# A four-layer graph network on one core: adjacency flag taken earlier, unit matrix from VectorE, weight preparation cut into four steps, output bias and the last norms on VectorE

## The reference, cut to what matters

```
L0: Wh = x W^T; e = leaky_relu(s1_i + s2_j), masked by adj == 0; softmax(e) @ Wh
L1: h = x W; logits = Ax_j + Ay_i + h a12 h^T; leaky_relu, masked by adj > 0; softmax @ x
    elu(x W1 + (softmax @ x) W2)
L2: 4 heads; q, k, v = x W + b; mask = adj | eye; softmax(q k^T * scale) @ v; relu(out @ Wo + bo)
L3: relational graph convolution over relation numbers 1 to 40: relu(sum_r (adj == r) @ ((h + b_r) * sigmoid(g + bg_r)))
```

## Time and profile before

| | |
|---|---|
| median of 3 runs | 518.59 us (518.09 to 518.69) |
| the profiled execution's own time | 518.74 us |
| its span, first to last instruction | 516.9 us |
| PE, PEld, DVE, ACT, POOL busy | 478.7, 411.4, 397.7, 425.1, 317.7 us |

### The profile page before, as it was taken

How to read it: one execution, slowest core, us unless ns; L and a number is a source line. 1 busy time by engine, 2 the same in 40 slices (tenths; PEclk the granted TensorE clock), 3 DMA queues, 4 the chain that set the end, 5 groups by cost and what they waited for, 6 DMA issues and landing times. The chain is left out here.

```text
span 516.9 us, 14050 instructions
## 1 busy us (share of the span) xinstructions
PE 478.7 (93%) x3964; PEld 411.4 (80%) x3964; DVE 397.7 (77%) x1558; ACT 425.1 (82%) x1261; POOL 317.7 (61%) x717
## 2 busy tenths in 40 slices
PE   3767899999999999999999999999999999999880
PEld 2556788888888898888888888888888888888660
DVE  3486788889888888889888888888987888766540
ACT  2444999989988888999898888898998988898740
POOL 3054456566766766666666676766676676664562
PEclk9988999999999999999999999999999999999996
DMA  6121101122122211222122221122212200000111
GB/s 188 30 83 41 42 13 53 53 63 61 55 63 62 62 44 37 58 63 63 52 64 62 63 58 31 49 63 62 63 52 64 62 23 22 22 22 22 32 32 30
DMA packets 40220, 26.92 MB, mean 52 GB/s; under 512 B 2641, under 2 KB 39889, under 8 KB 40146
## 3 DMA queue, kind: packets, MB, share of 16 engines
q1 hardware_dynamic: 40146, 26.03, 17.4%
HBM read 17.63 MB, written 8.39 MB: 50 GB/s over the span
## 5 line engine op out<-in xcount | busy, mean ns | idle before, releaser
L744 ACT ACTIVATE p<-p,nmax 128x256 f32<-128x256 f32 x256 | 126.6, 498 | 0.4 <-DVE nmax L941 0.4
L1140 POOL TENSOR_SCALAR x<-y,minus_mean,rstd 128x128 f32<-128x128 f32 x256 | 114.7, 458 | 17.7 <-issue 15.9
L1122 POOL TENSOR_TENSOR rstd<-ve,minus_half 128x2 f32<-128x2 f32 x128 | 101.9, 796 | 0.0
L941 DVE CUSTOM_DVE_ANT_0 p<-ps,neg 128x256 f32<-128x256 f32 x256 | 92.7, 419 | 6.6 <-PE ps L520 6.6
L1115 POOL TENSOR_SCALAR ve<-stats 128x2 f32<-128x2 f32 x128 | 24.7, 193 | 110.8 <-DVE stats L854 105.6
L753 ACT COPY p2T<-ps 128x512 f32<-128x512 f32 x128 | 75.0, 595 | 0.0
L531 PE MATMUL ps<-ident,p 128*128 128x128 f32 x512 | 71.7, 273 | 1.5 <-ACT p L744 1.5
L531 PEld LDWEIGHTS ps<-ident,p 128*128 128x128 f32 x512 | 57.4, 141 | 3.2 <-DVE nmax L941 1.4
L977 DVE SCALAR_TENSOR_TENSOR y<-ps,x 128x256 f32<-128x256 f32 x32 | 13.7, 427 | 56.6 <-PE ps L576 56.6
L854 DVE BATCH_NORM_STATS2 stats<-y 128x6 f32<-128x256 f32 x128 | 53.2, 415 | 2.3
L662 ACT COPY xT<-ps 128x256 f32<-128x256 f32 x96 | 36.6, 382 | 17.6 <-PE ps L400 17.1
(11 more groups left out here) (134 smaller groups left out, 1232.3 us busy)
## 6 DMA issues: line engine op xcount, KB each, us to landing
adj_in<-in_adj_dram SPq DMA_DIRECT2D x32, 256.0 KB, 3.0
xT<-in_xT_dram SPq DMA_DIRECT2D x32, 128.0 KB, 2.8
x_in<-in_x_dram SPq DMA_DIRECT2D x32, 128.0 KB, 3.0
x_aside<-x SPq DMA_DIRECT2D x32, 128.0 KB, 2.2
out_dram<-x SPq DMA_DIRECT2D x32, 128.0 KB, 1.8
l_w<-in_l_w_dram SPq DMA_DIRECT2D x1, 257.0 KB
l_w<-in_l_w_dram SPq DMA_DIRECT2D x1, 256.0 KB
first_w<-in_first_w_dram SPq DMA_DIRECT2D x1, 129.0 KB, 2.2
```

Source lines behind the costliest of these rows:

```text
L744: last = nc.scalar.activation(p2(n)[:, k, a, :], p2(n)[:, k, a, :], ACT.Exp, bias=nmax2(n)[:, k, a:a + 1], scale=-1.0, accum_out=sum2(n)[: ...
L941: last = nc.vector.tensor_tensor_reduce(p2(n)[:, k, a, :], bank("sc2", n, a)[:, k * N:(k + 1) * N], neg2(n)[:, k, :], -1.0, HIGHEST, ALU.a ...
L1122: nc.gpsimd.tensor_tensor(rstd[layer](n), ve[layer](n), minus_half[:, :], ALU.pow)\
L1140: last = nc.gpsimd.tensor_scalar(dst[:, k, 0:D], y_t[layer](n)[:, k, :], minus_mean[layer](n)[:, k:k + 1], rstd[layer](n)[:, k:k + 1], ALU ...
```

## The change

- DVE makes `ident`: a row of numbers 0 to 127 from eight memsets and four additions, a product on TensorE that spreads it, and a comparison. `lift` follows on DVE, `not_eye` on POOL from `ident`. The zero rows are cleared on POOL.
- `setup_later` is cut into `prep_a` to `prep_d` (TensorE) and `c_prep_a` to `c_prep_d` (ScalarE), with places of their own. `tT(0)`, `xw1(0)` wait for their results.
- `load` on SP is cut into `ld_xT`, `ld_adj`, `ld_w`, `ld_x`; the weights come ahead of graph 1.
- `bo` is added by DVE: `y2` becomes `y2a` (bank + `bo_row`) and `y2b` (relu and residual). The bf16 products of `wo2` and `setup_biases` are gone.
- `masks` is cut into `masks` (L0) and `neg1`. For the last three graphs, norms 2 and 3 are done on DVE (`end_norm2`, `end_norm3`).
- The flag is computed after `eq1(31)`: DVE `flag_a`, a product with ones on TensorE (`flag`), DVE `flag_b`. POOL's reduction is gone.
- All places in `PLAN` are new: `proj0` at 10694 and `agg3` at 17075 are 6.4 rounds apart. Ring `adj` 3 to 5, `eq1` 8 to 7.

```diff
 PLAN (new; steps of TensorE, ScalarE and GpSimd, and DVE)
+    "tensor": [("proj0", 10694), ("s2_rows", 10909), ("prep_a", 11545), ("pT0", 11559), ("prep_c", 11587),
+        ("agg0", 11591), ("prep_b", 11950), ("prep_d", 12017), ("xT1", 12109), ("tT", 12346), ("z1", 12576),
+        ("pT1", 12901), ("xw1", 13189), ("agg1", 13331), ("xT2", 13690), ("qk2", 13768), ("sc2", 13807),
+        ("pT2b1", 14236), ("v2", 14366), ("pT2a0", 14532), ("pT2b0", 14535), ("pT2a1", 14544), ("rs_rows", 14853),
+        ("agg2", 15034), ("wo2", 15329), ("xT3", 16364), ("hg3", 16806), ("agg3", 17075), ("flag", 15122)],
+    "scalar": [("c_proj0", 10868), ("c_s2", 11052), ("exp0", 11297), ("c_prep_a", 11621), ("c_pT0", 11639),
+        ("c_prep_c", 11695), ("c_prep_d", 12090), ("c_xT1", 12144), ("c_tT", 12315), ("relu1", 12724),
+        ("c_prep_b", 12783), ("exp1", 12944), ("c_pT1", 13008), ("c_xw1", 13181), ("c_elu1", 13268),
+        ("c_xT2", 13773), ("c_qk2", 13848), ("exp2b", 14128), ("exp2a", 14255), ("c_v2", 14440), ("c_pT2a0", 14693),
+        ("c_pT2b0", 14740), ("c_pT2a1", 14787), ("c_pT2b1", 14809), ("c_rs", 14944), ("c_xT3", 16481),
+        ("gate3", 16914)],
+    "vector": [("neg1", 10631), ("masks", 10935), ("e0", 11223), ("m0", 11295), ("s0", 11682), ("r0", 11806),
+        ("y0", 11811), ("b0", 11917), ("e1", 12655), ("r1", 13388), ("h1", 13390), ("y1a", 13403), ("y1b", 13415),
+        ("b1", 13501), ("e2b", 14087), ("e2a", 14161), ("r2", 14456), ("eq1", 14622), ("onT2", 15244),
+        ("y2a", 15378), ("y2b", 15614), ("b2", 15828), ("end_norm2", 16267), ("vals3", 17028), ("y3", 17318),
+        ("b3", 17955), ("end_norm3", 18990), ("flag_a", 14623), ("flag_b", 15622)],
+    "gpsimd": [("var0", 11827), ("rsq0", 11921), ("norm0", 12075), ("neg2", 13292), ("var1", 13386), ("rsq1", 13489),
+        ("norm1", 13573), ("rs_rep", 14785), ("var2", 15915), ("rsq2", 16034), ("norm2", 16145), ("var3", 18247),
+        ("rsq3", 18331), ("norm3", 19216)],
 DVE, setup
+                for k in range(8):
+                    last = nc.vector.memset(index[:, k:k + 1], float(k))
+                for k, size in enumerate((8, 16, 32, 64)):
+                    last = nc.vector.tensor_scalar(index[:, size:2 * size], index[:, 0:size], float(size), None, ALU.add)
+                nc.vector.tensor_tensor(ident[:, :], index[:, :], ps[:, 3, 0:P], ALU.is_equal)\
 TensorE
+                pe.matmul(ps[:, 3, 0:P], index[0:1, :], ones_row[:, :], start=True, stop=True)\
 wo2 and y2
-                    pe.matmul(o[:, k * D:(k + 1) * D], onT(n)[:, k * P:(k + 1) * P], l2_w[:, WO],
-                              start=True, stop=False)
-                    last = pe.matmul(o[:, k * D:(k + 1) * D], ones_bf[:, :], bo_parts[:, :],
-                                     start=False, stop=True)
+                    last = pe.matmul(o[:, k * D:(k + 1) * D], onT(n)[:, k * P:(k + 1) * P], l2_w[:, WO],
+                                     start=True, stop=True)
-                nc.vector.scalar_tensor_tensor(out=y_t[2](n), in0=o, scalar=0.0, in1=x2(n)[:, :, 0:D], op0=ALU.max, op1=ALU.add)\
+                nc.vector.tensor_tensor(y_t[2](n), o, bo_row[:, :].rearrange("p (t d) -> p t d", t=1)
+                                        .to_broadcast([P, T, D]), ALU.add).then_inc(sem("y2a_ready"), 1)
+                nc.vector.scalar_tensor_tensor(out=y_t[2](n), in0=y_t[2](n), scalar=0.0, in1=x2(n)[:, :, 0:D],
+                                               op0=ALU.max, op1=ALU.add).then_inc(sem("y2_ready"), 1)
 the end
-            pool.wait_ge(sem("excess_ready"), 1)
-            nc.gpsimd.partition_all_reduce(excess_all[:, :], excess_max[:, :], P, bass.bass_isa.ReduceOp.max)\
-                .then_inc(sem("excess_all_ready"), 1)
```

More of the change, by code:

```diff
@@ L26 @@
 PLAN = {
-    "sync": [("load", -56), ("aside", 7895), ("store", 10433)],
[15 rows of a table removed]
+    "sync": [("ld_xT", 9787), ("ld_adj", 10173), ("ld_w", 10463), ("ld_x", 11423), ("aside", 16293),
+        ("store", 18816)],
[6 rows of a table added]
+        ("c_prep_c", 11695), ("c_prep_d", 12090), ("c_xT1", 12144), ("c_tT", 12315), ("relu1", 12724),
[12 rows of a table added]
 }
 RING = {
[1 row of a table removed]
[1 row of a table added]
     "x1": 3, "xT1": 2, "tT": 2, "xw1": 3, "relu": 2, "p1": 2, "p1T": 2, "h": 2, "hexp": 2,
@@ L51 @@
 }
-FIRST_BANK = {"a": 0, "b": 4}
-WEIGHTS_AFTER = 0
+BANKS = {"a": (0, 1, 2, 3), "b": (4, 5, 6, 7)}
+AT_END = 3
+GRAPHS = {
+    **{step: (0, 1) for step in ("ld_w", "prep_a", "prep_b", "prep_c", "prep_d",
+                                 "c_prep_a", "c_prep_b", "c_prep_c", "c_prep_d")},
+    **{step: (-1, 0) for step in ("flag_a", "flag", "flag_b")},
+    **{step: (0, -AT_END) for step in ("norm2", "norm3")},
+    **{step: (-AT_END, 0) for step in ("end_norm2", "end_norm3")},
+}
 PSUM_USES = {
@@ L79 @@
     "agg2": [("b", "onT_sb")],
-    "wo2": [("b", "y2_ready")],
+    "wo2": [("b", "y2a_ready")],
     "xT3": [("b", "xT_sb3")],
@@ L83, with graphs_of @@
     "agg3": [("b", "y3_ready")],
-}
+    "prep_a": [], "prep_b": [], "prep_c": [], "prep_d": [],
+    "flag": [("b", "flag_ready")],
+}
+def graphs_of(step, graphs):
+    first, end = GRAPHS.get(step, (0, 0))
+    return range(first if first >= 0 else graphs + first, end if end > 0 else graphs + end)
 def program(engine, graphs):
@@ L90, in program @@
             sorted((place + 1000 * n, k, name, n)
-                   for k, (name, place) in enumerate(PLAN[engine]) for n in range(graphs))]
+                   for k, (name, place) in enumerate(PLAN[engine]) for n in graphs_of(name, graphs))]
 def psum_table(graphs):
-    table, rings = {}, {r: [] for r in FIRST_BANK}
+    table, rings = {}, {r: [] for r in BANKS}
     for step, n in program("tensor", graphs):
         for k, (ring, *_) in enumerate(PSUM_USES[step]):
-            uses = rings[ring]
-            table[step, n, k] = (FIRST_BANK[ring] + len(uses) % 4, uses[-4] if len(uses) >= 4 else None)
+            uses, banks = rings[ring], BANKS[ring]
+            table[step, n, k] = (banks[len(uses) % len(banks)],
+                                 uses[-len(banks)] if len(uses) >= len(banks) else None)
             uses.append((step, n, k))
@@ L306, in _, with ld_adj @@
         def _(sp):
-            def load(n):
+            def ld_adj(n):
                 if n >= RING["adj"]:
@@ L330, in _ @@
             sp.dma_start(first_w[:, :], t["first_w"]).then_inc(sem("w0_loaded"), 16)
-            run("sync", {"load": load, "aside": aside, "store": store})
+            run("sync", {"ld_adj": ld_adj, "ld_xT": ld_xT, "ld_x": ld_x, "ld_w": ld_w, "aside": aside, "store": store})
             for s in range(RING["x4"]):
@@ L443, in s2_rows @@
                 last.then_inc(sem("s2_ps"), 1)
-                if n == 0:
-                    setup_later()
             def rs_rows(n):
@@ L875, in s0 @@
             def s0(n):
-                if n == 0:
-                    setup_biases()
                 dve.wait_ge(sem("agg_ps0"), n + 1)
@@ L957, in onT2, with y2a @@
                     .then_inc(sem("onT_sb"), 1)
-            def y2(n):
+            def y2a(n):
                 dve.wait_ge(sem("wo_ps"), n + 1)
@@ new lines, in end_norm @@
+            def end_norm(layer, n):
+                dve.wait_ge(sem(f"mean{layer}_ready"), n + 1)
+                dve.wait_ge(sem(f"rstd{layer}_ready"), n + 1)
+                dst = (x3, x4)[layer - 2](n)
+                if layer == 2:
+                    free(dve, "x3", n, "y3_ready")
+                    if n >= RING["x3"]:
+                        dve.wait_ge(sem(f"x3_aside{n % RING['x3']}"), 16 * (n // RING["x3"]))
+                if layer == 3 and n >= RING["x4"]:
+                    dve.wait_ge(sem(f"stored{n % RING['x4']}"), 16 * (n // RING["x4"]))
+                if n == B - AT_END:
+                    dve.wait_ge(sem(f"x{layer + 1}_ready"), n)
+                for k in range(T):
+                    last = nc.vector.tensor_scalar(dst[:, k, 0:D], y_t[layer](n)[:, k, :],
+                                                   minus_mean[layer](n)[:, k:k + 1], rstd[layer](n)[:, k:k + 1],
+                                                   ALU.add, ALU.mult)
+                last.then_inc(sem(f"x{layer + 1}_ready"), 1)
@@ new lines, in flag_a, with flag_b @@
+            def flag_a(n):
+                dve.wait_ge(sem("eq1_ready"), B)
+                nc.vector.tensor_reduce(excess_max[:, :], excess_col[:, :], AX.X, ALU.max)\
+                    .then_inc(sem("excess_ready"), 1)
+                dve.wait_ge(sem("excess_ready"), 1)
+                nc.vector.tensor_scalar(excess[:, :], excess_max[:, :], 1.0, None, ALU.is_gt)\
+                    .then_inc(sem("excess_ready"), 1)
+            def flag_b(n):
+                dve.wait_ge(sem("excess_ps"), 1)
+                nc.vector.tensor_scalar(excess_flag[:, :], bank("flag", n)[0:1, 0:1], 0.5, None, ALU.is_gt)\
+                    .then_inc(sem("flag_ready"), 1)
@@ L981, in _ @@
```

(3 more changed lines are left out.)

169 lines of the change are left out of this document (85 added, 84 removed), and 17 rows, old and new, of tables (PLAN, RING).

## The result

| | before | after |
|---|---|---|
| median of the runs | 518.64 us (518.09 to 518.99) | 543.39 us (540.62 to 545.47) |
| profiled execution | 518.74 us, span 516.9 | 544.33 us, span 542.5 |

The changed kernel takes 1.0475 times as long, with an interval of 1.0424 to 1.0526. The prediction was 513.2 us with a range up to 522: it had the wrong sign. The runs of the changed kernel lie within 0.9%, more than the 0.2% of before; the difference is five times that.

A forecast was written before the change was run, and what follows sets the result against it. PE was taken to bound the kernel, the time being its work plus its idle time. Output bias -5.8, head -6.4, middle +10.8 and tail -4.1 sum to -5.5: 518.7 to 513.2 us, range 503 to 522.

The forecast's parts named there:

- Middle: PE's rounds from 61 to 478 us: new order adds 0.40 us of waits a graph, +10.8 us (+6.5 to +13.8).
- a part of 0.1: Middle: waits of `pT1` behind `exp1` and `agg1` behind `c_xw1` give some 0.1 us more.
- The round worked out at 14.76 us: Middle: one round carried through three queues, 14.76 us against 14.25 of work, 0.5 of waits.
- Output bias: `wo2` in each graph: two bf16 products leave PE, 0.18 us over 32 graphs, -5.8 us.
- Head: Kernel's start: earlier `ident`, `setup_later` in gaps, no `setup_biases`; -6.4 us, bounds -11.9 and 0.
- Its first half: Start up to `xT1(0)`: it moves from 29.56 to about 17.6; PE's idle time falls by 10.0 us.
- +3.6: Head after `xT1(0)`: the less deep order makes PE wait 9 us, 3.6 more than before.
- Tail: Kernel's end: last store ends it -4.7, DVE norms -0.6, shallower order +1.2; -4.1 us, bounds -6.6 and -2.5.
- -0.6: Tail: two norms on the last graph's path save 0.5 us each on DVE, less 0.43 for `y2b`.
- C: Rival, waits win: `neg2` and `m0` meet, a round loses 0.8 us instead of 0.4; 524.0 us, chance 0.21.
- D: Rival, head gives nothing: POOL's 7.43 us come at its first ordinary operation, preparation blocks PE; 519.6 us, chance 0.10.
- B: Rival, PE stays full: the middle's waits are absorbed; 502.4 up to 509 us, chance 0.21.

The follow-up runs named there:

- experiment 1: The changed kernel with all its parts, but the old places and old rings (`adj` 3, `eq1` 8): 503.83 us, ratio 0.9724.
- experiments 3 to 6: Changed kernel: PE work into gaps before `qk2`, `sc2` (580.2 us); also `neg2` moved (579.48); `xw1` before previous graph's `sc2` (576.68); that plus first move (603.65).
- experiment 7: The changed kernel with VectorE's side work (`r2`, `eq1`, `neg1`) moved out of the stretch between `agg1` and `xT2`: 540.07 us, ratio 1.0387.
- experiment 11: The kernel before with the output bias alone moved from two TensorE products to one VectorE addition: 513.8 us, ratio 0.9862.
- experiment 9: The changed kernel with one more, unused GpSimd operation in each graph's norm of layer 1: 557.3 us, ratio 1.0735.
- experiment 12: The kernel before with the flag alone changed, a TensorE product and comparisons replacing GpSimd's reduction at the end: 512.85 us, ratio 0.9870.
- experiment 8: Changed kernel's parts in the old places, with the last three graphs' norms of layers 2 and 3 on GpSimd again: 502.01 us, ratio 0.9672.
- experiment 2: The changed kernel with GpSimd's `neg2` moved behind `norm1`, so it no longer runs beside `m0` on VectorE: 544.02 us, ratio 1.0492.

## Why the prediction was wrong

**Middle, "I take 0.40": the step that failed.** It measured +31.9 us, 31 rounds of 1.03 us more each (15.29 less the 14.26 that experiment 1 has with the same parts), where +10.8 was forecast, 27 rounds of 0.40. The parts of the term were read rightly: `xT2` to `qk2` takes 0.96 us (0.97 forecast, 0.66 offered), the norm comes 6.27 us behind `agg1` (6.3), the waits appear where they were named. The error is in how they were put together. I took each loop by itself against the PE work beside it, and the floor as the largest single shortage. An estimate shows what that left out: the distances of the same steps in experiment 1 give PE about 5.9, 0.66, 1.8 and 5.9 us of work in the four legs, which measure 6.26, 0.96, 1.90 and 6.16, so about 0.35, 0.3, 0.1 and 0.3 us of waiting, one behind the other. The last of them had gone into the forecast as a part of 0.1. For in the new order these loops are links of one ring: `agg1(n)`, norm, `xT2(n)`, `qk2(n)`, `sc2(n)`, softmax of the scores, `agg1(n+1)`. Its last link is new. Before, `agg1(n+1)` is issued 3.11 us behind `sc2(n)`, ahead of everything that uses these scores. After, three steps stand ahead of it in PE's queue that can't run until VectorE or ScalarE has worked on the scores: `xw1` (bank), `pT2b1` (exponentials), `wo2` (behind `onT2` in DVE's order). Together that is 6.0 to 6.2 us, and 6.26 + 0.96 + 1.90 + 6.16 = 15.28 us is the round. PE's work of about 14.25 us does not set it. So the shifts of PE's work that were tried lost: experiments 3 to 6 each made two or three legs longer and shortened the last by 0.23 us at most, while taking work off the chain itself (experiment 7) gave back all that it took off. The round worked out at 14.76 us failed at this link. How much each of the three links alone would cost was not separated.

**Output bias, -5.8.** Right: 14.43 to 14.26 us a round (experiment 11), 0.17 x 31 = -5.3. DVE had the room.

**Head, -6.4.** It measured -2.6. Its first half was right, its second not. `xT1(0)` came at 19.55 instead of the 17.6 forecast and the 29.56 of before, with 6.9 us of PE's idle time up to there (6.0 forecast); `z1(0)` came 11.3 us earlier. But the first five rounds are 13.0 us longer, 4.3 of it the steady 0.86 us each; 8.7 more is, for the most part, that the short rounds of the filling are gone. Before, `z1(1)` follows 7.32 us behind `z1(0)`, with few graphs in flight; after, 14.50. I had put +3.6 there. From the second round on they are close to the steady one (14.84 to 15.12 us), as if the ring held them too; that was not tested. The first is another matter. In it the granted clock fell, and in experiment 9, with the same order and a longer chain, it did not. The same two windows of the changed kernel, then of experiment 9, with the columns of the earlier trace rows:

```profile
25.00:28.00 3.00, 0.84 (x6) 0.63 (x6) 1.81 (x6) 1.49 (x4) 1.80 (x5) 1.00 0.57 178
28.20:35.00 6.80, 5.31 (x16) 3.71 (x16) 2.92 (x10) 1.50 (x4) 1.20 (x2) 0.50 0.00 0
25.00:28.00 3.00, 0.85 (x6) 0.63 (x6) 1.78 (x6) 1.85 (x5) 1.43 (x4) 1.00 0.59 178
28.20:35.00 6.80, 3.71 (x22) 2.88 (x23) 4.45 (x12) 2.61 (x7) 2.17 (x6) 1.00 0.00 0
```

From 28.2 to 35.0 us the changed kernel ran at the lower of the clock's two levels (0.50), and its first round took 14.50 us; experiment 9 kept 1.00 and took 12.47, though PE was as little busy in the three microseconds before. Its first five rounds come to 74.47 us with 0.43 us more in each, so about 2.4 us of the 8.7 may be the clock, an estimate; the kernel before lost some in these rounds too (3.4 us at 0.50, from 46.4).

**Tail, -4.1.** It measured -0.7, and the last rounds before it shrink less (+2.3 us). The flag itself gave the 4.4 us that it was to give (4.7 forecast, experiment 12). Taken back were 2.4 us by the end norms (experiment 8, measured in the old order alone), for which I had counted -0.6 without asking what stands behind them in DVE's queue, and 1.1 us by a longer drain (49.1 us for experiment 1's 47.9), in which `xT2` and `pT2b1` of the last graph wait 2.46 and 1.42 us. The clock can account for that 1.1: it was 0.50 from 512.9 to 516.3 us, where `hg3` took 1.70 us for 1.03 and `sc2` 2.09 for 1.15, while before it fell only after PE's last product.

**Sum by the same terms.** -5.3 - 2.6 + 31.9 + 2.3 - 0.7 = +25.6 us, the difference of the spans.

**Rivals.** C and D had the sign, and C's price (0.8 us of waits a graph) was nearest, but for another reason. Its mechanism is real: the Trainium skill, "GPSIMD Engine Reference", section 1 (Specifications), lists SBUF interfaces shared with VectorE, with contention for VectorE instructions with two SBUF inputs, and the trace agrees with 0.41 us becoming 1.04 in the first half of `m0`. It had slack behind it (experiment 2). B and D are refuted: PE does not stay full, and POOL's 7.43 us do not come back at its first ordinary operation (`not_eye` starts at 3.97).

**The better kernel.** All the parts but the end norms, in the order and with the rings of before: 502.0 us, 3.3% under before and 7.6% under the changed kernel. An order that keeps the new places and cuts all three links was not tried.

## What to carry to other kernels

When an order is changed on an in-order engine, don't only compare each wait with the work beside it: follow one item's chain until it meets the next item's, add up the ring, and compare it with the round. If the ring passes through one round only, its sum is a floor whatever the engines' loads are; it is broken by issuing the next item's steps ahead of all those that depend on the item before. A delay of known size added at one point of two orders tells cheaply whether the point is on what sets the round: nearly all of it shows, or nearly none. It does not tell by which way the ring closes; for that, take work out of one leg and see whether the leg shrinks.

## What was not expected of the hardware

- GpSimd's stall of 7.43 us at the start belongs to the reduction over the partitions, though this is issued at the very end: with the reduction replaced and the affine selects kept (experiment 12), the first select starts at 1.84 instead of 9.05. Experiment 11, which keeps both, has it again (7.90 us of idle time, select at 9.51). What happens in it the traces don't show.
- VectorE's norm is shorter by itself (0.60 for 0.89 us), and the kernel still lost 2.4 us at its end by it: VectorE's queue stood up to 1.34 us for GpSimd's `rstd` (experiment 1), with `vals3` behind it.
- The runs of one kernel mostly differ as their granted clocks do. The changed kernel's four spans of 538.8, 540.7, 542.5 and 543.7 us have mean granted clocks of 0.996, 0.990, 0.988 and 0.985; those of experiment 8, 499.0, 499.5, 500.8 and 500.9 us, have 0.992, 0.992, 0.989 and 0.988. This spread is 0.9% at most and can't explain the 4.8%, but it can explain differences of 1 to 3 us between single profiles.
